# Last stage of a fused language-model tower: each token's router weight brought to its partition by TensorE transposes instead of VectorE products and sums

## The reference, cut to what matters

```python
def _L3_ffn_ref(x, attention_mask, wr, br, w1, b1, w2, b2):
    ...
    weights = (jnp.einsum('bsd,do->bso', x, wr) + br)[..., 0]
    k = max(1, int(CAPACITY * s))
    kk = k - 1 if k > 1 else 1
    _, idx = jax.lax.top_k(weights, k)
    sel_idx = idx[:, :kk]
    sel = jnp.take_along_axis(x, sel_idx[:, :, None], axis=1)
    h = jax.nn.gelu(jnp.einsum('bkd,dh->bkh', sel, w1) + b1)
    y = jnp.einsum('bkh,hd->bkd', h, w2) + b2
    w_sel = jnp.take_along_axis(weights, sel_idx, axis=1)
    y = y * w_sel[..., None]
    ...
    processed = jnp.zeros_like(x).at[batch_idx, sel_idx].set(y)
    return processed + x
...
    h = h + _L3_ffn_ref(_layernorm(h, axis=-1), L3_ffn_attention_mask, L3_ffn_wr, ...)
```

## Time and profile before

| | us |
|---|---|
| median of 3 runs | 812.21 |
| lowest, highest | 812.11, 816.56 |
| the profiled execution | 819.01 |
| its span, first to last instruction | 817.1 |

### The profile page before, as it was taken

One profiled execution on the slowest core, in us unless ns is written; L12 is line 12 of the kernel. 1 busy time (PEld: TensorE's weight loads), 2 busy tenths in 40 slices (PEclk: granted clock), 3 DMA queues, 4 the chain that ended last, 5 costly groups with the idle time before them and its releaser, 6 DMA issues. The chain is left out here.

```text
span 817.1 us, 13076 instructions
## 1 busy us (share of the span) xinstructions
PE 638.4 (78%) x4688; PEld 424.8 (52%) x4688; DVE 533.5 (65%) x1442; ACT 330.4 (40%) x638; POOL 245.2 (30%) x217
## 2 busy tenths in 40 slices
PE   3497565774889778999988999988787787998864
PEld 3365444653767442232267887876232224984653
DVE  1034789654374578778945888484848886843897
ACT  1032211352555545545514465321243289831542
POOL 6612911414030011001025766441300177300420
PEclk9688879787999765989989999697689889999987
DMA  6854430102000010000010000004000000000011
GB/s 209 272 157 109 119 85 1 68 2 56 1 0 2 1 69 1 0 2 1 0 36 7 13 13 8 12 2 129 0 1 1 19 16 1 2 4 1 0 27 26
DMA packets 18944, 30.05 MB, mean 37 GB/s; under 512 B 6466, under 2 KB 15810, under 8 KB 18242
## 3 DMA queue, kind: packets, MB, share of 16 engines
q1 hardware_dynamic: 16322, 19.80, 8.7%
q0 software_dynamic: 2560, 9.44, 3.7%
HBM read 27.25 MB, written 1.05 MB: 35 GB/s over the span
## 5 line engine op out<-in xcount | busy, mean ns | idle before, releaser
L166 POOL TENSOR_TENSOR norm_rstd<-norm_var,minus_half 128x16 f32<-128x16 f32 x16 | 47.2, 2953 | 323.7 <-DVE norm_var L160 323.7
L1309 ACT ACTIVATE m_g<-PS,w_slot 128x512 f32<-128x512 f32 x96 | 60.8, 685 | 72.8 <-PE PS L1363 72.7
L1363 PE MATMUL PS<-m_xT,w_slot 64*128 64x512 f32 x192 | 71.5, 699 | 6.4 <-ACT m_g L1309 6.3
L1251 DVE TENSOR_TENSOR m_gw<-m_g,PS 128x512 f32<-128x512 f32 x96 | 61.0, 676 | 18.7 <-PE PS L1371 9.2
L1387 PE MATMUL PS<-m_gw,w_slot 128*64 128x512 f32 x192 | 58.1, 675 | 1.2 <-DVE m_gw L1251 1.2
L106 PE MATMUL PS<-w_base 128*128 128x128 f32 x316 | 45.8, 299 | 7.9 <-PEq L2737 7.2
L106 PEld LDWEIGHTS PS<-w_base 128*128 128x128 f32 x316 | 40.0, 156 | 12.4 <-issue 10.7
L267 PE MATMUL PS<-w_base,tok_windows 128*128 128x128 f32 x128 | 22.0, 334 | 24.3 <-issue 12.2
L328 DVE COPY tok_windowsT<-PS 128x512 f32<-128x512 f32 x16 | 11.1, 691 | 41.9 <-remote 22.0
L1371 PE MATMUL PS<-m_gT,m_sel 48*128 48x512 bf16 x96 | 24.3, 421 | 17.1 <-DVE m_gw L1251 11.4
L2151 ACT COPY rat_xf<-PS 64x512 f32<-64x512 f32 x32 | 33.3, 1042 | 9.0 <-PE PS L2204 8.6
(11 more groups left out here) (341 smaller groups left out, 1635.6 us busy)
## 6 DMA issues: line engine op xcount, KB each, us to landing
rff_routed<-in_routed SPq DMA_DIRECT2D x64, 129.0 KB, 2.0
w_slot<-in_w_rat SPq DMA_DIRECT2D x1, 1525.0 KB, 11.2
w_slot<-in_w_win SPq DMA_DIRECT2D x1, 1378.5 KB, 5.8
w_slot<-in_w_m SPq DMA_DIRECT2D x1, 1329.0 KB, 5.7
w_slot<-in_w_early SPq DMA_DIRECT2D x1, 1092.0 KB
rat_inv<-in_rat_taps SPq DMA_DIRECT2D x1, 1024.0 KB, 7.4
rat_hf<-in_rat_taps SPq DMA_DIRECT2D x1, 1024.0 KB, 7.5
out<-H SPq DMA_DIRECT2D x8, 128.0 KB, 2.2
```

Of the source, the lines that this page charges most:

```text
L166: nc.gpsimd.tensor_tensor(N.rstd[:], N.var[:], C.minus_half[:], ALU.pow).then_inc(S["norm_rstd"], 1)
L1251: nc.vector.tensor_tensor(gw[:, i % 2, half, :], g[:, i % 2, half, :], gate_bank[half], ALU.mult)\
L1309: nc.scalar.activation(g[:, i % 2, half, :], hid_bank[(n - 1) % 3], ACT.Gelu, bias=b1[:, s:s + 1])\
L1363: nc.tensor.matmul(hid_bank[n % 3], w1[lane(half), s, :], pair_of(xT, pair)[lane(half)], start=True, stop=True).then_inc(S["hid_ps"], 1)
```

## The change

The tensor `own` and VectorE's products and sums are gone. Instead TensorE transposes, for each group `k` of a chunk, 32 of the 128 equal rows of `wb` (a float32 block of 32 partitions x 128) against a 32x32 piece of the identity. The result is 128 partitions x 32 equal columns, and lies in columns `32 k` to `32 k + 31` of bank 1, the bank that ScalarE has just emptied. VectorE copies the first column of each of the four groups to `wn` (128x4), with the semaphores `wn_ps` and `wn`. Since bank 1 is now taken until that copy is made, the hidden layer's second half (`s = 1`) moves behind the transposes of all four chunks, and waits for `wn` of its chunk. The order of the four small copies ahead of all comparisons stays.

```diff
@@ depth_ffn
-                        "stored h_plus_x wb own wn compared rank taken scale y_ps ys h_new xT_ps xT wb_ps hid0_ps "
+                        "stored h_plus_x wb wn_ps wn compared rank taken scale y_ps ys h_new xT_ps xT wb_ps hid0_ps "
...
-        own = sb("own", [P, W, 2 * U, P])
...
                 for w in range(W):
-                    v.wait_ge(S["wb"], it * W + w + 1)
-                    nc.vector.tensor_tensor(own[:, w], wb[:, w], bcast(C["ident"], 1, 2 * U), ALU.mult)\
-                        .then_inc(S["own"], 1)
-                for w in range(W):
-                    v.wait_ge(S["own"], it * W + w + 1)
-                    nc.vector.tensor_reduce(wn[:, w], own[:, w], AX, ALU.add).then_inc(S["wn"], 1)
+                    v.wait_ge(S["wn_ps"], it * W + w + 1)
+                    nc.vector.tensor_copy(wn[:, w], PS[w][:, 1, 0:2 * U * ROWS].rearrange("p (k r) -> p k r", r=ROWS)[:, :, 0])\
+                        .then_inc(S["wn"], 1)
...
-                for w in range(W):
-                    for s in range(SLABS):
-                        if s == 1:
-                            pe.wait_ge(S["wb"], it * W + w + 1)
-                        for half in range(2):
-                            ins = nc.tensor.matmul(PS[w][:, s, half * T:(half + 1) * T], w1[:, s, half, :], xT[:, w],
-                                                   start=True, stop=True)
-                        ins.then_inc(S["hid0_ps"] if s == 0 else S["hid1_ps"], 1)
+                def hidden(w, s):
+                    for half in range(2):
+                        ins = nc.tensor.matmul(PS[w][:, s, half * T:(half + 1) * T], w1[:, s, half, :], xT[:, w],
+                                               start=True, stop=True)
+                    ins.then_inc(S["hid0_ps"] if s == 0 else S["hid1_ps"], 1)
+
+                for w in range(W):
+                    hidden(w, 0)
+                    pe.wait_ge(S["wb"], it * W + w + 1)
+                    for k in range(2 * U):
+                        ins = nc.tensor.transpose(PS[w][:, 1, k * ROWS:(k + 1) * ROWS], wb[0:ROWS, w, k, :],
+                                                  ident[0:ROWS, 0:ROWS])
+                    ins.then_inc(S["wn_ps"], 1)
+                for w in range(W):
+                    pe.wait_ge(S["wn"], it * W + w + 1)
+                    hidden(w, 1)
```

More of the change, by code:

```diff
@@ L2277 @@
 SLABS = HID3 // P
+ROWS = 32
 def depth_ffn(nc, H, PS, C, dram):
```

## The result

The changed kernel is slower by 0.42% (ratio to the kernel before 1.0042, 95% interval 1.0029 to 1.0055). Its median of 14 runs is 817.31 us (812.27 to 818.94), that of the kernel before 813.58 (14 runs, 812.11 to 816.68): 3.4 us by the ratio (2.4 to 4.5). The forecast was +3.3 us. The time itself came out above the 815.5 us forecast and above its own range of 814.2 to 816.7: the sum was added to 812.21, the median of three runs, where 14 runs of the kernel before give 813.58.

What follows compares the result with a forecast made beforehand. VectorE's path from the last `wb` to the first comparison was taken to bound the kernel; TensorE's queue would delay that by 1.66 and 1.65 us. Added to 812.21, +3.3 us gave 815.5 us, own range 814.2 to 816.7, overall 811.8 to 819.0.

Steps and rivals of the forecast that it cites:

- The edge: VectorE's first comparison per round: its start moves the end equally, and would follow TensorE's order instead of the arrival of `wb`.
- The size: Delay of the first comparison: 5.56 us after the first hidden product, so 1.66 and 1.65 us later in the two rounds.
- The first-half products: Hidden layer on TensorE, ahead of the last transposes: 16 records at 0.216 us, 3.46 us per round.
- the transposes: 0.110 us each: TensorE's 16 new transposes per round: 0.110 us pitch taken, bounds 0.03 and 0.142; 15 x 0.110 to the sixteenth's start.
- the copy, taken at 0.16: VectorE's copy of the fourth chunk's 128x4 weights from PSUM, ahead of the first comparison: 0.16 us.
- The rule on weight loads: Skill rule for TensorE: a load costs by columns, 107 ns for 128; by it the sum would be about +3.2 us.
- The cover: TensorE's second-round result ahead of VectorE's use at `ys`: shrinks from 4.7 to 4.5 us, so the edit costs nothing there.
- ScalarE's bunched GELUs: ScalarE waits for the first second-half product until about 774.8, then does seven GELUs by 779.7, while TensorE still works.
- The clock did not fall among the transposes: Rival: TensorE's clock halves among the hidden layer's transposes, giving 820.7 us for one round, or about 825; chance 0.05.
- The moved slow stretch: Rival: TensorE's half-clock stretch between rounds shifts, gaining or losing 1.7 us, so 813.8 or 817.2 us; chance 0.14.
- Transposes nearly free: Rival: 32 rows and columns make load and product short on TensorE; sum +0.9 us, 813.1 us; chance 0.12.
- transposes as early as `wb`: Rival: transposes do not queue behind the first half; comparisons 2.2 us earlier per round, 807.8 us; chance 0.04.

Runs made afterwards that it cites:

- e1: The change with the transposes of all four chunks ahead of the hidden layer's first half; ratio 0.9929 to the kernel before.
- e4: The kernel before, VectorE's products and sums kept, only the hidden layer reordered to all first halves, then all second halves; ratio 1.0000.
- e5: The change, plus 44 transposes of the identity on TensorE in its gap between the two rounds; ratio 1.0026 to the kernel before.
- e7: The change, but VectorE does chunk 0's comparisons ahead of the copies of chunks 1 to 3; ratio 0.9968 to the kernel before.
- e9: The kernel before, without transposes, with VectorE doing product, sum and comparisons chunk by chunk; ratio 0.9990.
- e2: The change with each transpose made twice into the same columns; ratio 1.0080 to the kernel before.
- e10: The change with transposes of 64x128 instead of 32x128; one execution, 823.8 us beside 820.3 of the kernel before, no ratio.
- e3: The change with whole 128x128 transposes instead of 32x128; ratio 1.0046 to the kernel before.
- e8: The change with transposes ahead of the hidden layer, chunk 0's comparisons ahead of the other copies, and 12 identity transposes between rounds; ratio 0.9907 to the kernel before.

## Why the prediction was right

**The edge.** It said that the start of the first comparison decides, and that after the change this start follows TensorE's list, not the arrival of `wb`. The chain shows it, and e1 confirms it by moving the same transposes forward.

**The size.** Forecast were +1.66 and +1.65 us from the first hidden product to the first comparison; measured +1.87 and +1.86. The first-half products took the forecast 0.216 us a record. The term that was mis-sized is the transposes: 0.110 us each, 0.44 per chunk, against 0.56 per chunk measured. It was wrong in kind as well. The transposes themselves follow each other at 0.0625 us, between the two rows that bounded them. The choice of 0.110 over 0.03 rested on a product with 16 moving columns and 128 rows; it did not carry over to transposes of 32 rows, though they too have 128 weight columns. What was left out is the passing between whole products and transposes of a part of the rows, about 0.3 us per chunk, of which the trace of the kernel before already had examples (0.32 us from L2437 to L2445 for 0.216). Up to the start of the sixteenth transpose the first error is 15 x 0.0475 = 0.7 us too much, the second some 1.0 too little (the sixteenth starts 5.4 us after the first product, less 3.46 and 15 x 0.0625); the copy, taken at 0.16, held up the first comparison by only 0.08 (768.67 and 768.75). That these errors nearly cancelled, at +0.2 us a round, is luck; that the transposes wait behind the first-half products, 3.46 us of the 5.56, is not. The rule on weight loads (the Trainium skill, "TensorE: Matmul & The Clock Gate", section "LDWEIGHTS (loading the stationary operand)", by its formula 107 ns for 128 columns) does not set the pitch of these transposes: they follow each other at 0.0625 us with 128 columns of weights. The 62 ns that the Trainium skill gives in the same page's "Back-to-back issue gap" for narrow operands where the sequencer decodes would fit the 0.0625, for 32 and for 64 columns; that this is the reason no run here shows.

**The cover.** TensorE's result was to stay 4.5 us ahead of `ys` in the second round; it is 808.61 - 804.28 = 4.33. No wait appeared there, ScalarE's bunched GELUs cost nothing, and e4 shows the same without transposes.

**The rivals.** The clock did not fall among the transposes: it is 1.00 from the first hidden product to the last result in both rounds. Of the two stretches below, the first is the head of the second round:

```profile
783.00:788.80 5.80, 5.78 (x18) 4.92 (x19) 3.64 (x11) 2.54 (x6) 4.86 (x4) 0.50 0.20 44
788.90:804.30 15.40, 15.39 (x95) 11.54 (x94) 8.84 (x49) 9.51 (x16) 0.00 (x0) 1.00 0.07 16
```

The rule that transposes do not count for the clock (the Trainium skill, same page, "Part 4: PE-mode transpose") finds no support here: in e5 44 float32 transposes kept it at full, 1.00 from 780 to 792. The moved slow stretch did occur: half speed from the round's first transpose on for 5.8 us, where before it was 4.2, and it cost 0.77 us in the profiled execution, within the 1.7 given to it. Transposes nearly free, and transposes as early as `wb`, did not happen; the latter is what e1 builds, and the price given to it, 4.4 us below the kernel before, lies within the interval of the 5.8 us measured (4.1 to 7.5).

**The sum.** 3.3 us were forecast, 3.4 measured (2.4 to 4.5). The profiled stage shows 4.5, of which 3.7 are the queue and 0.8 the clock. That the ratio lies below the 4.5 may be a smaller share of the clock in other executions; this was not separated. The 4.5 itself lies at the edge of the interval.

## What to carry to other kernels

Work taken off a busy engine pays only if that engine does not then wait for the replacement longer than it worked; on an engine that runs its list in order, that is decided by what stands ahead of it, so put the small piece that another engine waits for in front of the large ones that nobody waits for. Here this alone turned +0.4% into -0.7%. Where one consumer takes several chunks, let it start on the first rather than collect them all (e7; with the products and sums still on VectorE the same order gave nothing clear, e9). And take the price of an operation from a row of the same kind and shape, the passing to and from it included.

## What the runs showed of the hardware

- Float32 transposes with 128 columns of weights followed each other at 0.0625 us with 32 rows and moving columns (e2) and at 0.06 with 64 (e10), and at 0.109 with 128 (e3). The first two of a group of four stood further apart: from the first start to the last it took 0.21 us with 32 rows (0.43 - 0.22) and 0.24 with 64 (0.46 - 0.22).
- Between whole float32 products and transposes that use 32 or 64 rows some 0.3 us per pair of passings were lost; the first product record behind them reads 0.483 us instead of 0.379. With 128 rows nothing was lost (e3). In the kernel before, a passing cost about 0.1 us where the rows went from 128 to 64 or the weight columns from 128 to 64, and nothing where only the moving columns changed.
- 44 transposes of the identity, and nothing else on TensorE, held the granted clock at 1.00 over a gap of some 6 us, in which it fell to 0.50 in the kernel before and in the changed one. In e8, where the gap was 2.1 us (781.77 to 783.84), 12 of them went with a clock of 1.00 from 768 to 805 us.
